# Storing weight pieces from ScalarE's DMA queue in the recurrence of a decoder layer

## What is computed

```python
x = x + attn(layernorm(x))         # a linear recurrence over 4 steps: z = V (A z + u_t), output 2 Re z
x = x + xattn(layernorm(x), ctx)   # 16 heads, 77 keys and values from ctx (4, 77, 512)
x = x + ffn(layernorm(x))
# ffn: h = butterfly(x @ W_exp + b_exp); h = gelu(h + up_bias); y = butterfly(h) @ W_con + b_con + down_bias
```

## Time and profile before

| | |
|---|---|
| runs shown | 2257.61, 2257.93, 2251.99 us |
| profiled execution, its time | 2253.37 us |
| its span, first to last instruction | 2251.6 us |
| mean granted TensorE clock | 0.992 |
| ScalarE busy in the span | 1230.1 us, 55% |
| VectorE busy in the span | 1701.6 us, 76% |
| DMA, whole span | 443.35 MB, mean 197 GB/s |

### The profile page before, as it was taken

One profiled execution on the slowest core, in us unless ns is written; L12 is line 12 of the kernel. 1 busy time (PEld: TensorE's weight loads), 2 busy tenths in 40 slices (PEclk: granted clock), 3 DMA queues, 4 the chain that ended last, 5 costly groups with the idle time before them and its releaser, 6 DMA issues.

```text
span 2251.6 us, 41276 instructions
## 1 busy us (share of the span) xinstructions
PE 2211.9 (98%) x15960; PEld 1937.9 (86%) x15960; DVE 1701.6 (76%) x2854; ACT 1230.1 (55%) x2735; POOL 467.5 (21%) x578
## 2 busy tenths in 40 slices
PE   8999889999999999999999999999999999999999
PEld 6788678888888888789989989989989989889899
DVE  6776688888888888867957858758669678579467
ACT  3665567666666766635535436436346355355343
POOL 3530222232222232200210300300300300300203
PEclk8999999999999999999999999999999999999999
DMA  9999623323323322476686786786686776766765
GB/s 320 350 355 317 204 78 113 104 93 114 123 85 117 116 95 76 148 261 186 215 265 177 222 267 177 221 268 206 191 269 208 220 233 211 246 206 213 226 188 194
DMA packets 202091, 443.35 MB, mean 197 GB/s; under 512 B 32442, under 2 KB 70586, under 8 KB 200362
## 3 DMA queue, kind: packets, MB, share of 16 engines
q1 hardware_dynamic: 201898, 440.72, 60.7%
HBM read 341.66 MB, written 99.01 MB: 196 GB/s over the span
## 4 chain that ended last, share of the span: by engine, by line
PE 87%; DVE 5%; ACT 5%; DMA 1%; issue 1%; SPq 1%; DVEq 0%; ACTq 0%
PE ps L442 70%; PE ps L1990 5%; PE ps L1958 4%; PE ps L1969 2%; ACT es L1086 2%; PE ps L1921 1%; PE ps L1809 1%; ACT wc_h L1042 1%; PE ps L1878 1%; DMA wd_scratch<-stage 1%; PE ps L1860 1%; DVE rsum L1493 1%; DVE st L1278 1%; DVE xt2l L1315 1%; DVE ql L1315 1%
## 5 line engine op out<-in xcount | busy, mean ns | idle before, releaser
L442 PE MATMUL ps<-ring,gh 128*128 128x256 f32 x3584 | 652.8, 285 | 0.1
L442 PEld LDWEIGHTS ps<-ring,gh 128*128 128x128 f32 x3584 | 558.9, 192 | 2.1 <-DVE gl L1315 1.5
L442 PE MATMUL ps<-xth,ring 128*128 128x512 f32 x1792 | 553.3, 389 | 0.0
L442 PE MATMUL ps<-ring,gl 128*128 128x256 f32 x1792 | 507.5, 283 | 0.0
L442 PEld LDWEIGHTS ps<-xth,ring 128*128 128x128 f32 x1792 | 336.6, 188 | 69.5
L1183 ACT ACTIVATE gh<-G 128x512 fp32r<-128x512 f32 x384 | 239.2, 629 | 218.8 <-PE ps L442 218.3
L442 PE MATMUL ps<-xtl,ring 128*128 128x512 f32 x896 | 348.9, 389 | 0.0
L442 PEld LDWEIGHTS ps<-ring,gl 128*128 128x128 f32 x1792 | 344.0, 192 | 0.0
L1315 DVE TENSOR_TENSOR gl<-G,gh 128x512 fp32r<-128x512 f32 x384 | 275.6, 729 | 51.5 <-ACT gh L1183 50.5
L867 POOL TENSOR_TENSOR es<-es,rinv 128x308 f32<-128x308 f32 x256 | 180.4, 735 | 383.9 <-DVE rinv L1497 383.9
L1166 ACT ACTIVATE G<-G,up_b 128x512 f32<-128x512 f32 x192 | 138.9, 724 | 221.9 <-DVE G L1609 221.9
(11 more groups left out here) (234 smaller groups left out, 4379.1 us busy)
## 6 DMA issues: line engine op xcount, KB each, us to landing
ring<-wup_scratch SPq DMA_DIRECT2D x224, 512.0 KB, 3.8
ring<-wdn_scratch SPq DMA_DIRECT2D x224, 512.0 KB, 3.6
X<-x_scratch SPq DMA_DIRECT2D x32, 1024.0 KB, 8.7
xa<-in_x SPq DMA_DIRECT2D x16, 1024.0 KB, 8.7
x_scratch<-xa SPq DMA_DIRECT2D x16, 1024.0 KB, 10.4
x<-x_scratch SPq DMA_DIRECT2D x16, 1024.0 KB, 5.6
x_scratch<-x SPq DMA_DIRECT2D x16, 1024.0 KB, 4.3
out_x<-X SPq DMA_DIRECT2D x15, 1024.0 KB, 6.3
```

What stands on the lines that cost most here:

```text
L442: mm = pe.matmul(bank, a, b, start=first and i == 0, stop=last and i == n - 1, skip_group_check=go_on)
```

## The change

piece_out moves from SyncE's stream to ScalarE's. SyncE no longer waits for copies and issues none of the 72 stores. ScalarE issues the store of piece n-1 just ahead of its wait for piece n (for TensorE and for the staging tile), and the last one after the loop. The destinations, sizes and semaphores stay. The loads of the bias rows (bias_rows) stay on SyncE.

```diff
@@ SyncE @@
-            def piece_out(n):
-                sp.wait_ge(piece_act, n + 1)
-                src, out = stage[n % STAGES], stage_out[n % STAGES]
-                if n < BL:
-                    sp.dma_start(wl_d[P * (n - LU):P * (n - LU + 1)], src[:, :]).then_inc(out, 16)
...
@@
                     for n in pieces_at(g, c):
-                        piece_out(n)
                         bias_rows(n)
@@ ScalarE @@
+            def piece_out(n):
+                act.wait_ge(piece_act, n + 1)
+                src, out = stage[n % STAGES], stage_out[n % STAGES]
+                if n < BL:
+                    act.dma_start(wl_d[P * (n - LU):P * (n - LU + 1)], src[:, :]).then_inc(out, 16)
...
             def piece_back(n):
+                if n:
+                    piece_out(n - 1)
                 act.wait_ge(piece_pe, n + 1)
                 bank = ps[:, 6 + n % 2, :]
                 after(act, stage_out[n % STAGES], 16 * (n // STAGES))
@@
                         for o in range(KC):
                             hi_pre(xt2h[:, o, :], o)
+            piece_out(PIECES - 1)
             for c in range(KC):
                 hi_pre(woh[:, c, :], KC + c)
```

More of the change, by code:

```diff
@@ L974, in _ @@
             key_hi(3)
+            def piece_out(n):
[3 more added lines that the diff above has]
+                    act.dma_start(wl_d[P * (n - LU):P * (n - LU + 1)], src[:, :]).then_inc(out, 16)
+                elif n < DH:
+                    act.dma_start(b_d[0][n - BL:n - BL + 1], src[0:1, :]).then_inc(out, 16)
+                elif n < UH:
+                    act.dma_start(wh_d.rearrange("(p j) n -> j p n", j=MC)[n - DH], src[:, :]).then_inc(out, 16)
+                elif n < BH:
+                    act.dma_start(wu_d[n - UH], src[:, :]).then_inc(out, 16)
+                elif n < DL:
+                    act.dma_start(b_d[1][n - BH:n - BH + 1], src[0:1, :]).then_inc(out, 16)
+                else:
+                    act.dma_start(wd_d.rearrange("j (c l) n -> c l j n", c=MC)[n - DL], src[:, :]).then_inc(out, 16)
             def piece_back(n):
+                if n:
+                    piece_out(n - 1)
                 act.wait_ge(piece_pe, n + 1)
```

## The result

The changed kernel takes 2262.41 us in the median of 12 runs (2257.08 to 2266.32), the kernel before 2255.27 us in 12 (2250.61 to 2257.93). The ratio is 1.0031, with a 95% interval of 1.0023 to 1.0039: slower by 7.1 us, just at the 0.3% that I had set as the bound of what can be told. I forecast 3.5 us faster. The measured time lies inside the range, the sign is wrong. The profiled execution took 2262.74 us around a span of 2260.9 us, so it is near the median, and its trace may be read for the whole difference; its span is 9.3 us longer than that of before, whose profiled execution lay 1.9 us under its median.

The account below looks back on a forecast made before the run. In the recurrence it took TensorE's order of work and the transfers as both full. Terms of -2 (x1 load), -0.9 (staging), -0.6 (middle) and 0 (issues) gave -3.5 us: 2249.9 profiled, 2254.1 median; range from 3 us below 2249.3 to 2263.

Parts of the forecast that it names:

- part one: Recurrence's tail: SyncE, freed of 72 waits and issues, moves the x1 load by -4 to +3.7 us; -2 taken.
- The upper end: x1 load in the tail: five pieces stored beside it, 1.31 MB at 354 GB/s, delay it by 3.7 us.
- The hole: Low DMA share at 214 to 220 us, during the 4-byte load, read as room for the pieces' stores.
- The rule that I had named: DMA engines alternate queues packet by packet, so 2 KB rows would stretch the 4-byte load: the +3.7 us end.
- the lag should shrink: SyncE's x1 store of group 12, issued 5.9 us late, would lag only 2 or 3 us without the pieces.
- Part two: Tail: ScalarE's wait for a stored staging buffer before 233.13 us disappears, winning 0.9 us, or 0 at the other end.
- Part three: ScalarE's 72 issues and waits in the groups cost nothing, covered by its idle time; upper bound 14 us.
- Rival (c): Steady groups: ScalarE becomes the bound, +14 us less 3.5 at 0.9 us per issue, 2268.1 us; chance 0.15.
- Part four: Groups up to 136.06 us: rows of x could arrive earlier, 0 to -1.3 us; -0.6 taken.
- Rival (b): Transfers decide: same bytes on full engines, x1 rows later, 0 to +3.7 us, 2257.6 to 2261.3; chance 0.24.
- Rival (a): Whole tail comes free: query products at 230 us, -7 there and -1.3 in the middle, 2249.3 us; chance 0.19.
- Wrong by (b): Sign that transfers decide: x1 statistics start at 225 us or later although the x1 load was issued earlier.

Follow-up runs that it names:

- e3: Changed kernel with the last 16 pieces' stores back on SyncE's queue, the first 56 staying on ScalarE's: 2253.79 us, ratio 0.9995 to the kernel before.
- e4: Kernel with only the last 16 pieces' stores on ScalarE's queue, the first 56 on SyncE's: 2269.38 us, ratio 1.0060 to the kernel before.
- e10: No 4-byte load (bias computed as columns), first 56 pieces on ScalarE's queue, last 16 on SyncE's: 2253.93 us, ratio 0.9993 to the kernel before.
- e9: No 4-byte load (bias computed as columns), last 16 pieces on ScalarE's queue, first 56 on SyncE's: 2258.57 us, ratio 1.0016 to the kernel before.
- e6: Changed kernel without the 4-byte load (bias computed as columns), all pieces on ScalarE's queue: 2257.29 us, ratio 1.0006 to the kernel before.
- e8: Kernel before plus 72 issues of 64-byte transfers on ScalarE, each waiting for its own copy; pieces stay on SyncE: 2257.37 us, ratio 1.0002.
- e7: Changed kernel with SyncE keeping its 72 waits for the copies but issuing nothing for them: 2263.99 us, ratio 1.0034 to the kernel before.
- e11: A second profile of e6, no edit: this execution took 2257.34 us.
- e2: Changed kernel with the 4-byte bias load issued one chunk later, behind the first x1 load: 2256.21 us, ratio 1.0006 to the kernel before.
- e1: Kernel before with the 4-byte bias load issued one chunk later, behind the first x1 load: 2255.01 us, ratio 0.9996.
- e5: Kernel before without the 4-byte load (bias computed as columns), pieces on SyncE: 2252.61 us, ratio 0.9984.

## Why the prediction was wrong

**The step that failed is part one, the x1 load.** I gave it -4 to +3.7 us and took -2, "because the share of 0.2 to 0.5 during the 4-byte load says that the engines have room just there". It measured +6.46 us, outside both ends: 2.46 us because the x1 store ahead was complete later, and 4.0 us because the load itself took 17.4 us and not 13.4.

The upper end failed in its rate. It priced five pieces by their bytes, 1.31 MB at 354 GB/s, on top of transfers that keep their pace. But the pace fell: with both queues at work the engines moved 202 GB/s at a share of 0.52 to 0.54 from 214 to 218 us. The last 16 pieces stand on about eight engines, take every second turn there, and SyncE's transfers wait for that half while the other eight have nothing left to do. The choice of -2 failed in its reason. The hole was read as free room; it was the 4-byte load itself, many short packets, and a second queue gets its turns out of them: from 9.7 us to 26.9 us, ahead of the x1 load on the same queue.

What is shown, and what is not: the last 16 pieces on ScalarE's queue carry the loss (e3 0.9995, the change 1.0031, e4 1.0060; without the load e10 0.9993 and e9 1.0016). The traces of the change and of e4 show the x1 store, the 4-byte load and the x1 load behind it stretched; in e6 the x1 load takes 10.6 us again. How much of the time is the 4-byte load's doing is not settled: 0.28 of 0.60% when only the last 16 pieces move (e4, e9), 0.09 of 0.31% and within the noise when all move. That the eight engines are the reason is read from the shares and not tested: no run gave these stores another pattern. They are the only pieces whose destination is written as 8 by 16 rows; the other large ones have 128.

The rule that I had named as speaking against it was right, and I gave it too little. The Trainium skill (DMA: Bandwidth & Descriptors, section on queues, rings and completion order) has each DMA engine take turns between the queues with work, a packet at a time. The trace agrees: 196 beside 196 from 218 to 220 us. The page counts a packet as some 9 to 17 descriptors; the trace's records, single elements and single rows, change places one for one. I used the rule only to choose an end of a range made from bytes. It should have been a term of its own, in packets.

**Also in part one,** "the lag should shrink": it did in part, to 200.16 from 201.55 us for the x1 store and by 8.5 us for the 4-byte load. It bought nothing, since the x1 load waits for the store to be complete. I counted the issue and left out the wait behind it. The store, now beside the pieces and the 4-byte load, took 13.23 us, at most 9.4 before.

**Part two, the staging wait,** was right and worthless. ScalarE never waits for a stored buffer in the changed kernel; the 0.9 us that I took were swallowed, since TensorE waited for x1 anyway.

**Part three, the issues on ScalarE, at nothing,** was right as far as the runs show. I expected 0.4 to 0.8 us each. The two patterns that took SyncE 0.61 and 0.91 us take ScalarE 0.33 and 0.59 us in the median, so one is below that. The tile stage (duration in ns, minimum, median, maximum):

```profile
L967 ACTq DMA_DIRECT2D whigh_scratch<-stage x16: 326/326/372, 110.7 to 145.4; - x16
...
L973 ACTq DMA_DIRECT2D wd_scratch<-stage x16: 587/588/681, 197.3 to 244.8; - x16
```

They can start while an ACTIVATE runs, as assumed; ScalarE's timeline:

```profile
155.76 0.82 ACT L919 ACTIVATE xn<-xa,nmr,rstd 128x512 f32<-128x512 f32 x1 [1.57 <-POOL nmr L742]
155.77 0.33 ACTq L969 DMA_DIRECT2D wu_scratch<-stage  x1
```

e8 agrees for 72 shorter issues with their waits. Rival (c), slower by ScalarE, gave nearly the right direction for a cause that isn't there. Its rule in the Trainium skill (Perfetto Trace Analysis, the section on HWDGE DMA instructions), one sequencer at a time, would have made ScalarE's issues wait while SyncE's 7.25 us issue was open from 213.41. Four of ScalarE's start in that time, and each takes 0.59 us. Long ones do occur, 1.52 to 2.39 us in e4, e7, e9 and e11, but none of them while an issue of SyncE was open. So the rule does not show as a lock over the whole of a long issue.

**Part four, the middle, -0.6 us,** had the wrong sign. Group 14 starts 0.9 us later in the profile and 2.4 us later in the mean of the profiles.

**Rival (b), transfers decide, 0 to +3.7 us,** was the right kind with too small a price. My argument against it, "the hole at 214 to 220 us", speaks for it: the hole was full of packets. **Rival (a), the tail free at 230 us,** fell with every version: the earliest query products came at 235.48 us (e2). The floor left out that the x1 load can't go out before the x1 store of group 12 is complete, at 211.68 us at the earliest (e2).

**My signs to look for** did their work. "Wrong by (b): the statistics of x1 start at 225 or later although L597 was issued earlier" half came true: they start at 230.82, and the load was issued later. The sum as measured in the profile: x1 rows +6.46, half-clock transposes +1.7, in all 8.38 us by the first scores, to which the middle's late groups, the staging and the issues add nothing; the medians differ by 7.1 us.

## What to carry to other kernels

Before a transfer moves to another queue, list what the old queue holds beside it, and price the sharing in packets rather than bytes: a load of 2048 elements of 4 bytes is the one that suffers most, and whatever stands behind it on its queue or waits for a completion there suffers with it. Look also at the share that the moved transfer reaches on its own. If that is a half, as here, the other queue is slowed on that half of the engines and is soon idle on the rest. A low DMA share is room only if neither small packets nor such a half is its cause. A small-element load in the way is better taken out (here by computing the bias in the layout in which it is used, 0.16% faster). Moving it by one place gave most of the loss back in the changed kernel (e2) and nothing in the old one (e1); in both the stall went to the next item.

## What the runs showed of the hardware

Two things were not expected. First, the long issue wanders. The 4-byte load itself is issued in 0.36 to 1.54 us, and the next DMA of the same queue stands: 7.76 us before and 7.25 us after for the x1 load, 8.23 us for a piece in e1, 11.24 us for an x1 store in e2. In the kernels without that load (e5, e6, e9 to e11) SyncE's longest issue from 200 to 230 us is 5.39 us, that of a load of keys.

Second, two queues that both have large packets don't always fill the engines. From 212 to 216 us both queues of the changed kernel have data, 2 KB packets nearly all, one for one, at 187 GB/s, where one queue reached 354 from 160 to 180. The DMA view of these 4 us:

```profile
DMA packets 382, 0.75 MB, mean 187 GB/s; under 512 B 17, under 2 KB 17, under 8 KB 382
...
q10 hardware_dynamic: 191, 0.36, 26.6%
q1 hardware_dynamic: 191, 0.38, 25.3%
```

In the mean 8.4 packets are under way at once, where from 204 to 208 us it is 16.8. So about eight of the 16 engines work, each for the two queues in turn, and the other eight stand idle, with q1's part of its transfers there done. The 4-byte packets are not the reason: e9 has none and shows DMA shares of 0.52, 0.51 and 0.52 in the three windows from 212 to 218 us, at 128 to 197 GB/s, just while its x1 store takes about 15 us. e6, with the same tail in its program, has 0.68, 0.80 and 1.02 there. This stretch on half the engines is the likely seat of what the last 16 pieces still cost in e9; why e6 and e9 differ in its length no run settles.

The same trace shows the turns singly. From 218 to 220 us each 2 KB packet takes 84 ns and is followed by one 4-byte packet of 9 ns, eight of each in about 86 ns.
